# Load order, rank placement, first gates and gathers of a two-stage convolution block on one core

## The reference

```
y    = mean(gn(x)); gate = softmax(y Wg + bg)              # 8 experts
h    = relu(y W1 + b1); s = h W2 + b2
x    = x + gn(x) * sigmoid(sum_e gate_e s_e)               # a scale per image and channel

xz   = silu(in_proj(gn(x)));  x_ssm, res, gate = split(xz)
xf   = silu(depthwise_conv3(x_ssm))
perm = argsort(score) for each of 2 heads                  # a fixed order of the 1024 tokens
y    = selective_scan(gather(xf, perm), dt, A, B, C)       # dt, B, C from xf, gathered too
y    = gather(y, inverse perm)
x    = x + silu(out_proj(y * silu(gate) + res))
```

## Time and profile before

| | us |
|---|---|
| median of 3 runs | 946.37 (946.17 to 948.2) |
| profiled execution | 940.44 |
| its span in the trace | 938.6 |

### The profile page before, as it was taken

How to read it: one execution, slowest core, us unless ns; L and a number is a source line. 1 busy time by engine, 2 the same in 40 slices (tenths; PEclk the granted TensorE clock), 3 DMA queues, 4 the chain that set the end, 5 groups by cost and what they waited for, 6 DMA issues and landing times.

```text
span 938.6 us, 10961 instructions
## 1 busy us (share of the span) xinstructions
PE 790.8 (84%) x3732; PEld 508.5 (54%) x3732; DVE 580.3 (62%) x1112; ACT 563.7 (60%) x1069; POOL 344.3 (37%) x292
## 2 busy tenths in 40 slices
PE   1104888568999999999999999999999999977896
PEld 0003554466456745684568456755765566644753
DVE  6884614483759456864777476837692769267824
ACT  4850648343776486648754785578567756653452
POOL 0001224066504850385028621862086307530150
PEclk9655898688999999999999999999999999989899
DMA  8920005914785476637673759373937292757132
GB/s 304 412 84 0 1 32 146 121 51 147 191 108 205 152 194 81 221 121 219 81 225 129 207 83 232 128 209 74 234 129 209 73 159 87 213 127 142 55 126 90
DMA packets 109816, 136.10 MB, mean 145 GB/s; under 512 B 40761, under 2 KB 90434, under 8 KB 109762
## 3 DMA queue, kind: packets, MB, share of 16 engines
q1 hardware_dynamic: 97474, 99.61, 43.2%
q0 software_dynamic: 12288, 35.80, 11.6%
HBM read 82.83 MB, written 53.61 MB: 145 GB/s over the span
## 4 chain that ended last, share of the span: by engine, by line
PE 58%; ACT 13%; POOL 8%; DVE 7%; issue 7%; DMA 6%; SPq 2%; POOLq 0%; DVEq 0%; ACTq 0%
PE pj L1192 25%; PE pj L1314 7%; ACT big L522 5%; PE st L1234 5%; PE pj L1255 5%; POOL xt_scratch L396 4%; PE tp L1209 4%; PE tp L1211 3%; POOL crow L410 3%; PE pj L1265 3%; ACT xf L505 2%; DMA crow<-cd_scratch 2%; ACT L522 2%; DMA crow<-yt_scratch,idx 2%; PE tp L1304 2%
## 5 line engine op out<-in xcount | busy, mean ns | idle before, releaser
L1192 PE MATMUL pj<-xb,inw 128*128 128x512 f32 x768 | 339.7, 597 | 4.2 <-POOL xb L378 4.2
L396 POOL DMA_INDIRECT xt_scratch<-stage,idx x128 | 173.2, 1353 | 339.0 <-issue 267.3
L1192 PEld LDWEIGHTS pj<-xb,inw 128*128 128x128 f32 x768 | 143.3, 191 | 171.4 <-issue 163.7
L410 POOL DMA_INDIRECT crow<-yt_scratch,idx x128 | 133.2, 1040 | 139.3 <-DMA yt_scratch<-rs 57.7
L902 DVE SCALAR_TENSOR_TENSOR xf<-xs,small,xf 128x1024 f32<-128x1024 f32 x64 | 81.6, 1284 | 131.5 <-ACT xf L498 130.3
L1314 PE MATMUL pj<-gt,outw 128*128 128x512 f32 x256 | 118.1, 593 | 0.6 <-DVE gt L1056 0.6
L1255 PE MATMUL pj<-xp,mblk 128*128 128x128 f32 x512 | 72.7, 287 | 23.2 <-ACT gt L572 15.7
L545 ACT COPY ch<-tp 128x256 f32<-128x256 f32 x128 | 42.8, 381 | 82.2 <-PE tp L1246 82.0
L1255 PEld LDWEIGHTS pj<-xp,mblk 128*128 128x128 f32 x512 | 65.8, 201 | 29.4 <-ACT gt L572 21.5
L534 ACT COPY stage<-tp 128x256 f32<-128x256 f32 x128 | 47.9, 374 | 55.0 <-PE tp L1211 52.3
L1062 DVE SCALAR_TENSOR_TENSOR xb<-xb,pcur,rs 128x1024 f32<-128x1024 f32 x32 | 41.0, 1284 | 60.3 <-ACT rs L603 60.3
(11 more groups left out here) (191 smaller groups left out, 1138.9 us busy)
## 6 DMA issues: line engine op xcount, KB each, us to landing
xb<-in_x SPq DMA_DIRECT2D x26, 1024.0 KB, 8.7
xp<-xt_scratch SPq DMA_DIRECT2D x8, 2048.0 KB, 11.9
crow<-cd_scratch SPq DMA_DIRECT2D x64, 256.0 KB, 12.5
yt_scratch<-rs SPq DMA_DIRECT2D x16, 1024.0 KB, 4.9
out<-xb SPq DMA_DIRECT2D x16, 1024.0 KB, 7.4
xp<-xt_scratch SPq DMA_DIRECT2D x8, 272.0 KB, 8.7
xt_scratch<-stage,idx POOLq DMA_INDIRECT x128
crow<-yt_scratch,idx POOLq DMA_INDIRECT x128, 2.8
```

The lines of the kernel that those rows point to most:

```text
L396: pool.indirect_dma_start(out=xt_d.ap(), out_offset=bass.IndirectOffsetOnAxis(ap=idx[:, k:k + 1], axis=0), in_=v(stage, (nt * H + h) * ROW ...
L410: pool.indirect_dma_start(out=v(crow, k * NB * P, (1, NB * P)), out_offset=None, in_=yt_d.ap()[0:(h + 1) * N], in_offset=bass.IndirectOffs ...
L1192: last = nc.tensor.matmul(o[:, :], v(inw, ct * 3 * C + col + ot * P, (1, P)), x_view(par, b, ct, nt * HALF, HALF), start=(ct == 0), stop=( ...
```

## The change

- SP issues the loads of the first three pairs and of pair 3 ahead of seven small parameter loads, pair 4 ahead of the weights.
- DVE takes the statistics of pairs 0 to 3 before its first rank. Three of 16 ranks remain among the statistics, three in the setup chain, three stand behind `take_params` ahead of the first convolution, and seven behind both convolutions of pair 0.
- The negation of the decay constants moves from the statistics' end behind the softmax wait; ACT takes the square root of the first variance ahead of those constants' exponential.
- POOL no longer waits for `params_ready`. Pair 0 is scaled from `prm` as soon as scale and shift are written (a new semaphore, `scale_ready`); the other pairs read `pcur` as before.
- The gates of pair 0 move from the stretch ahead of cycle 0 into cycle 0, where those of other pairs stand in theirs. In cycle 7 ACT takes two gates ahead of the decays and two behind them.
- POOL issues the gathers of head 1 without waiting for those of head 0, and waits for both at the end.

The core of the diff; the matching lines on PE drop `if i:` in `cycle` and the two `gate(0, ...)` calls ahead of it, and the counts of DVE's setup steps at the end of the file are renumbered:

```diff
-            load_for_statistics(0)
+            for k in range(XB):
+                load_for_statistics(k)
+            load_for_statistics(XB)
...
-            load_for_statistics(1)
+            load_for_statistics(XB + 1)
...
-            for k in range(2, PH):
+            for k in range(XB + 2, PH):
                 load_for_statistics(k)
...
-            pool.wait_ge(params_ready, 1)
...
-                hold(pcur_ready, i + 1)
+                if i:
+                    hold(pcur_ready, i + 1)
+                else:
+                    hold(scale_ready, 1)
...
+                    params = v(pcur if i else prm, (par * NB + b) * PRM_W, (1, PRM_W))
...
-                hold(y_gathered[h], 128 * (i + 1))
+                if h == H - 1:
+                    hold(y_gathered[0], 128 * (i + 1))
+                    hold(y_gathered[1], 128 * (i + 1))
...
                 turned(i, 0, range(0, AHEAD))
-                decays(i, 1)
-                if i:
+                if more:
+                    decays(i, 1)
                     gate(i, par, range(0, 4))
-                turned(i, 0, range(AHEAD, 4 + AHEAD))
+                else:
+                    gate(i, par, range(0, 2))
+                    decays(i, 1)
+                    turned(i, 0, range(AHEAD, 4))
+                    gate(i, par, range(2, 4))
+                turned(i, 0, range(AHEAD if more else 4, 4 + AHEAD))
...
             rows_out(0, 0)
-            gate(0, 0, range(0, 4))
             convolved(0, 1)
             rows_out(0, 1)
-            gate(0, 0, range(4, 8))
-            for b in range(NB):
-                for ct in range(CT):
-                    gate_again(0, b, ct)
...
             statistics(2)
+            statistics(3)
...
-            for i in range(3, PH):
-                for _ in range(1 if i == 3 else 2):
+            for i in range(4, PH):
+                if i > 4:
                     rank(*next(tiles))
                 statistics(i)
...
-            nc.vector.tensor_tensor(per_image(PRM_B), v(dts, 192, (B, CT), (1, B)), v(dts, 128, (B, CT), (1, B)), ALU.mult)
+            nc.vector.tensor_tensor(per_image(PRM_B), v(dts, 192, (B, CT), (1, B)), v(dts, 128, (B, CT), (1, B)), ALU.mult).then_inc(scale_ready, 1)
...
+            for _ in range(3):
+                rank(*next(tiles))
             convolve(0, 0)
+            convolve(0, 1)
             for tile in tiles:
                 rank(*tile)
...
-            convolve(0, 1)
             add_bias(0, 0, 0, NT)
```

More of the change, by code:

```diff
@@ L195, in build @@
         z_ready = sem("z_ready")
+        scale_ready = sem("scale_ready")
         out_ready = sem("out_ready")
@@ L376, in scale_x @@
                     hold(x_in[par][b], x_loads(i))
+                    params = v(pcur if i else prm, (par * NB + b) * PRM_W, (1, PRM_W))
                     for ct in range(CT):
                         last = nc.gpsimd.tensor_scalar(x_view(par, b, ct), x_view(par, b, ct),
-                                                       v(pcur, (par * NB + b) * PRM_W + PRM_P + ct, (1, 1)),
-                                                       v(pcur, (par * NB + b) * PRM_W + PRM_B + ct, (1, 1)), ALU.mult, ALU.add)
+                                                       params[:, PRM_P + ct:PRM_P + ct + 1],
+                                                       params[:, PRM_B + ct:PRM_B + ct + 1], ALU.mult, ALU.add)
                     last.then_inc(x_scaled, 1)
@@ L463, in _ @@
                 statistics(i)
+            act.wait_ge(setup_v, V_VAR1)
+            did(nc.scalar.activation(v(dts, 0, (1, 32)), v(dts, 0, (1, 32)), ACT.Sqrt))
             act.wait_ge(weights_in, 15 * 16)
             did(nc.scalar.activation(v(small, ANEG, (1, 16)), v(small, ANEG, (1, 16)), ACT.Exp))
-            act.wait_ge(setup_v, V_VAR1)
-            did(nc.scalar.activation(v(dts, 0, (1, 32)), v(dts, 0, (1, 32)), ACT.Sqrt))
             act.wait_ge(setup_v, V_MAX)
@@ L618, in cycle @@
                 result(i, 0, 1)
-                if i:
-                    gate(i, par, range(4, 6))
+                gate(i, par, range(4, 6))
                 results(i, 1)
-                if i:
-                    gate(i, par, range(6, 8), TURNED)
-                    for b in range(NB):
-                        for ct in range(CT):
-                            gate_again(i, b, ct)
+                gate(i, par, range(6, 8), TURNED)
+                for b in range(NB):
+                    for ct in range(CT):
+                        gate_again(i, b, ct)
                 if beyond:
@@ L798, in _ @@
             link(nc.vector.scalar_tensor_tensor(col(SQ), col(SQ), 0.25, col(T), ALU.mult, ALU.add))
-            dve.wait_ge(setup_a, 3)
-            link(nc.vector.tensor_scalar(v(small, ANEG, (1, 16)), v(small, ANEG, (1, 16)), -1.0, None, ALU.mult))
             dve.wait_ge(stats_done_a, PH)
@@ L832, in _ @@
             dve.wait_ge(setup_a, 5)
+            link(nc.vector.tensor_scalar(v(small, ANEG, (1, 16)), v(small, ANEG, (1, 16)), -1.0, None, ALU.mult))
             link(nc.vector.reciprocal(v(bc8, 142, (1, 1), parts=B), v(bc8, 141, (1, 1), parts=B)))
@@ L1340, in cycle @@
                 before_t = (t_drained, i * T_U + AHEAD)
-                if i:
-                    gate(i, par, range(0, 4), last)
-                    last = four(g_drained, i * G_U + 4)
+                gate(i, par, range(0, 4), last)
+                last = four(g_drained, i * G_U + 4)
                 results(i, 0, before_t, last, AHEAD, lambda: chunk_sums(i, 1, 0))
                 last = four(r_drained, i * R_U + 4)
-                if i:
-                    gate(i, par, range(4, 6), last)
-                    last[:2] = four(g_drained, i * G_U + 8)[:2]
+                gate(i, par, range(4, 6), last)
+                last[:2] = four(g_drained, i * G_U + 8)[:2]
                 chunk_sums(i, 1, 1)
@@ L1351, in cycle @@
                 last = four(r_drained, (i + 1) * R_U)
-                if i:
-                    gate(i, par, range(6, 8), last, TURNED)
-                    last[:2] = four(g_drained, (i + 1) * G_U)[2:]
+                gate(i, par, range(6, 8), last, TURNED)
+                last[:2] = four(g_drained, (i + 1) * G_U)[2:]
                 last = last[TURNED:] + last[:TURNED]
@@ L1376, in _ @@
             rows(0, 0, None)
-            gate(0, 0, range(0, 4), four(a_drained, A_U))
             rows(0, 1, (x_drained, NT))
-            gate(0, 0, range(4, 8), four(g_drained, 4))
-            project(1, 0, four(g_drained, G_U))
+            project(1, 0, four(a_drained, A_U))
             project(1, 1, four(a_drained, A_U + 4))
@@ L1389 @@
 V_MOB = 6
-V_STATS = 54
-V_VAR1 = 58
-V_Y = 62
-V_MAX = 65
-V_HID = 69
-V_HIDT = 70
-V_STATS2 = 85
-V_VAR2 = 89
+V_STATS = 47
+V_VAR1 = 51
+V_Y = 55
+V_MAX = 58
+V_HID = 63
+V_HIDT = 64
+V_STATS2 = 79
+V_VAR2 = 83
 V_DIAG = 35
-V_Q = 92
+V_Q = 86
 P_EXPERT = 4
```

2 lines of the change are left out of this document (1 added, 1 removed).

## The result

The changed kernel takes **933.04 us** (median of 4 runs, 930.54 to 937.82) against 946.27 (944.59 to 948.2): ratio 0.987 [0.984, 0.990], 13.2 us less. The forecast was 925.2 with a range of 920 to 932.5: the sign was right, the gain was to be 21.15, and the time lies 0.5 above the range.

A forecast was written before the change was run, and what follows sets the result against it. Prediction: PE bounds the middle cycles, so gains come only elsewhere: 8.7 (loads and statistics) - 0.2 + 2.85 (setup) + 4.9 (into cycle 1) + 4.9 (last cycles) = 21.15; 946.37 - 21.15 = 925.2 us, range 920 to 932.5.

The forecast's parts named there:

- the loads: Loads for the statistics: new order fills 1.9 us of DMA holes, so the last half pair lands at 52.5, not 54.4.
- the last cycles: Cycles 6 and 7: 4.9 us (3 to 6), with 4.0 from head 1's earlier gathers in cycle 6, then 0.4 and 0.5.
- first projection to cycle 1: Stretch into cycle 0: gates moved and ranks redistributed end cycle 0 at 256.4 instead of 261.24, 4.9 us.
- rival 1: Loads: small ones cost DMA time wherever they stand, only DVE's lag goes, 6.7 for 8.7: 927.2 us; chance 0.12.
- DVE's lag: Statistics: DVE, 6.7 us behind the data because of nine rank steps, would with three be as early as the data.
- Setup: Before the first projection: pair 0 scaled once scale and shift are ready, PE starts near 89.9 instead of 92.72, 2.85 us.
- rival 3: Cycle 0: no room for the gates, all eight units, 15.8 us, come on PE's path after crow: 941.0; chance 0.06.
- rival 2: Pair 1's scaling: POOL and DVE exclude each other, 2.6 us delays the first convolution and scatter: 927.8; chance 0.10.
- the 0.4: Cycle 7: two gates ahead of the decays, so PE need not wait for their drains once the weights block is ready.
- The 0.5: Cycle 7's last gathers: PE waits 0.61 us there, so no more can come; 0.5 taken.
- Rival 4: Gathers: 16 in one go stall in POOL's descriptor writing or full DMA engines, losing 4.5 us: 929.7; chance 0.05.
- Rival 5: Every cycle: head 1's gathers beside DVE's taps hold DVE, 7.5 us per cycle, 27 over six cycles: 952; chance 0.03.

The follow-up runs named there:

- e5: The kernel before, unaltered, run again for a second trace: median 947.13 us, ratio 1.0005.
- after: The first profiled execution of the changed kernel: 930.54 us, span 928.4; its timed median is 933.04.
- e1: The changed kernel run again, unaltered: median 934.89 us, ratio 0.9862 to the kernel before.
- e4: The changed kernel with ACT's statistics of pair 2 moved ahead of its four score-row copies: median 933.32 us.
- e8: The changed kernel with pair 0's scaling again waiting for params_ready instead of scale and shift: median 937.42 us, ratio 0.9914 to the kernel before.
- e11: The changed kernel a third time, unaltered, on one chip with e9 and e10: median 939.66 us, ratio 0.9916 to the kernel before.
- e7: The changed kernel with pair 0's gates back in front of cycle 0: median 940.26 us, ratio 0.9934 to the kernel before.
- e3: The kernel before with only both heads' gathers issued in one go: median 948.59 us against 947.22, ratio 1.0022.
- e9: The changed kernel with the old wait between the heads' gathers in cycles 6 and 7 alone: median 937.05 us, ratio 0.9889 to the kernel before.
- e10: e6 with one go in cycles 0 to 5 and the old gather wait in 6 and 7: 934.75 us, ratio 0.9867 to the kernel before.
- e12: The changed kernel with the loads in the old order: median 940.89 us, ratio 0.9906 to the kernel before.
- e6: The changed kernel with the old gather wait, ACT's pair 2 statistics earlier, the 8-value load first, weights behind the last x load: 928.66 us, ratio 0.9816.

## Why the prediction was wrong

The size failed in two terms, the loads and the last cycles. The trace of e5 is the better measure for the stages than the first one, whose last cycle is untypical; its execution (942.79) still lies 4.3 under its median. Against it the three traces of the changed kernel end 12.4 earlier (941.0 against a mean of 928.6). By the columns of the table: landing -0.2, landing to first projection 9.25, first projection to cycle 1 4.5 (mean of 162.17, 161.42 and 164.36 against 167.14), cycle 1 to the end -1.1.

- **Loads, 1.9 forecast, -0.2 measured: failed.** Two steps of the sum were wrong. First, 0.9 of the 1.9 was read as a hole at 50 to 52.5, but there the loads run out: the engines are full until 51 and then ebb. The same ebb stands ahead of the landing in `after` and e1. Windows of the kernel before:

```profile
50.50:51.00 0.50, 0.00 (x0) 0.00 (x0) 0.50 (x1) 0.50 (x1) 0.00 (x0) 0.50 0.98 385
51.00:51.50 0.50, 0.00 (x0) 0.00 (x0) 0.50 (x3) 0.39 (x2) 0.00 (x0) 0.50 0.60 238
```

  Second, "the small ones no longer leave a hole": they take their time at another place. From 10 to 15 the loads went from 275 to 421 GB/s; from 25 to 30 they fell from 420 to 237 in `after`, and to 327 in e1. By the traces' DMA records the packets of 8 to 136 bytes moved along: 857 at 10 to 15 before, 836 and 896 at 25 to 30 in `after` and e1. In `after` the engines are idle for a part of it (shares 0.91 and 0.66), in e1 they are nearly full and yet move less. Windows of the kernel before, then of e1:

```profile
25.00:27.50 2.50, 1.41 (x4) 0.34 (x2) 0.78 (x2) 1.06 (x3) 0.00 (x0) 1.00 1.03 421
27.50:30.00 2.50, 0.00 (x0) 0.00 (x0) 1.30 (x3) 2.50 (x6) 0.00 (x0) 1.00 1.02 419
...
25.00:27.50 2.50, 1.80 (x5) 0.49 (x3) 2.50 (x5) 0.66 (x2) 0.00 (x0) 1.00 1.06 292
27.50:30.00 2.50, 0.00 (x0) 0.00 (x0) 2.40 (x14) 2.50 (x6) 0.00 (x0) 1.00 0.94 361
```

  So rival 1 gave the number and, in the main, the reason. Waits on the statistics stand there too: pair 4's load (24.84) waits for DVE's statistics of pair 1, which stand behind the second head's scores (the first four of the twelve at 22.34, to 24.8), and pair 5's (34.54) for ACT's of pair 2. But e4, which sends pair 5's load 2.9 earlier, lands no earlier. (The prediction has six half pairs ahead of the small loads; it is eight, and the last two wait for pair 0's statistics.) With the weights behind the last load, the landing does come earlier (51.76, 50.52).
- **DVE's lag, 6.8 forecast (8.7 less the landing's 1.9), 6.66 measured: right** (7.98 to 1.32 behind the landing).
- **Setup: right.** Scaling 2.97 (e8) for 2.85; the chain got longer by 0.4, not 0.2 (9.25 is 6.66 + 2.97 - 0.4).
- **First projection to cycle 1, 4.9 forecast, 4.5 measured: right in size, the parts not.** In the times of before (9.11 later, the difference of the first projections) the scatter starts at 130.15 (121.04 + 9.11) for 129.9 forecast. It then lost 2.5, not 0.3, beside taps, those of pair 1, and ACT's third copies, which waited 7.17 for it, began at 154.9 for 152.4. The crow load lands at 181.8 for 182.9, and DVE waits 2.40, not 7. The sentence that the gates cost nothing in cycle 0 holds; rival 3 (15.8 on PE's path) does not: PE's wait for the first weights block fell from 7.49 to 0.61, and cycle 0 takes 88.82, 88.74 and 91.02 with the gates (`after`, e1, e11), 89.06 without them in e7, and 89.39 and 87.11 in the kernel before. PE is busier by about 9 us there, at a granted clock of 0.91 for 0.83. Windows of cycle 0 in the kernel before, in `after` and in e7:

```profile
171.85:261.24 89.39, 71.75 (x365) 53.24 (x366) 55.45 (x96) 44.07 (x85) 43.03 (x36) 0.83 0.49 118
...
156.96:245.78 88.82, 80.68 (x397) 54.13 (x397) 55.24 (x96) 52.59 (x97) 46.06 (x36) 0.91 0.50 127
...
164.77:253.83 89.06, 71.17 (x364) 52.39 (x365) 55.33 (x96) 43.93 (x85) 44.63 (x36) 0.83 0.41 115
```

  So the gain is the gates', in the stretch ahead of cycle 0 that they left (e7).
- **POOL and DVE beside each other (rival 2): there, but hidden.** While POOL scales pair 1, two of DVE's three L785 take 0.53 and 1.11 where they take 0.35 elsewhere (so in all traces with ranks there, but for e8, which scales later), and POOL's four take 5.01 instead of 4.72:

```profile
84.84 0.53 DVE L785 SCALAR_TENSOR_TENSOR mblk<-crow,m,ch 128x128 f32<-128x128 f32 x1
...
86.75 1.11 DVE L785 SCALAR_TENSOR_TENSOR mblk<-crow,m,ch 128x128 f32<-128x128 f32 x1
...
91.58 2.61 DVE L906 SCALAR_TENSOR_TENSOR xf<-xs,small,xf 128x1024 f32<-128x1024 f32 x2 [1.71 <-ACT xf L505]
```

  DVE is idle for another 1.71 behind it, so 0.9 us of stretch costs nothing. The Trainium skill (SBUF — State Buffer, section "SBUF: two separate sides") has the two exclude each other for a whole instruction; the trace agrees in kind for these two, and the neighbouring L786 (0.34) was not held.
- **The last cycles, 4.9 forecast, -1.1 measured against e5: failed; this is the larger part.** The step "in cycle 6 ... I take 4.0 of the 4.52" holds for the gathers' start (4.3), not for what follows. In eight of eight traces with one go in cycle 6, DVE learns of PE's first turns 5.8 to 7.4 late, in six of six with the old wait within 0.4. From cycle 6's first L1224 to its first output pass 91.38 and 91.40 with one go (`after`, e1), 91.62 and 91.08 with the old wait (before, e5): what the earlier gathers win, the late signals take. Alone on the kernel before, one go costs 1.4 (e3). In cycle 7 the 0.4 came: PE's first products stand 34.53 behind the cycle's first row in `after`, 34.75 and 34.92 before, and follow the weights block at once. The 0.5 could not come: head 1's gathers there wait for head 1's store of y, in `after` (POOL's timeline) as in e5; the 4.46 of the earlier trace rows is the first trace's alone.

```profile
891.54 0.94 POOL L416 DMA_INDIRECT crow<-yt_scratch,idx  x1 [8.17 <-DMA yt_scratch<-rs]
```

  Rival 4 came near (929.7) with another mechanism: POOL's descriptor writing did not stall (0.94 to 0.95 for each gather of cycle 6).
- **The base: untypical, at a small price.** The sum was made against 940.44, and its cycle 7 was read for the 0.4 and 0.5 of the last term; the 0.5 fell with it. The trace is 4.1 us shorter in its tail than e5's. Carrying the 5.93 to the median kept the forecast's level right. But the gain between the two first traces (10.2) understates the change for that reason, and cycle 7's own loss looked like the change's.

Rival 5 (gathers hold DVE in every cycle) and a loss in the middle cycles did not come: 96.95. Of the prediction's signs of being wrong, the landing behind 54.4 came (54.52 and 55.02, but 53.26 in e1). The taps start 7.97, 7.74 and 7.33 behind the first projection, on both sides of its 7.6, as the two traces of the kernel before do (7.62 and 7.41).

**Open.** Why PE's signals come late. In `after` the eight turns of 806.88 and the four projections behind them end by 810, and their semaphore events appear together at 814.0 to 814.1, while landings of the gathers are recorded all through this time. In all eight traces with one go in cycle 6 DVE's late L1053 starts 0.1 to 1.7 us behind the last recorded landing of head 1's gathers, so by the records the signal came only when these were done. The ends of PE's rows in a trace are modelled, so a signal that came late and work that ended late look alike here. Cycle 3 takes 97.8 to 102.1 in every trace but the first of before, which has 96.94; in e9 ACT's copies and drains again run behind PE there. That is part of the spread between executions: e7, e9, e10 and e12, with 100.0 and more in it, have the four longest tails of the table. All these traces hold fewer semaphore events (6,620 to 7,448) than the first of before (9,484), and those with one go in cycles 0 to 5 the fewest (6,620 to 6,856). The Trainium skill (NOTIFIC — the notification-queue block, section "7.1 Overflow: three behaviours, one of which stalls the engine") says that the path of the profile's records can hold back an engine; no run here shows whether that is what happened. Also open is why the changed kernel spreads more by chip (933 to 940) than the kernel before (946 to 949).

## What to carry to other kernels

A wait that is taken away moves an edge; follow the edge to the next instruction that uses it, also in the stretch where it should be won, and price the stretch alone (here: the one edit on the kernel before) before it goes into a sum. Before a sum is made against one trace, take a second one and compare them stage by stage. How far an execution lies from the median does not tell: the first trace's lies 5.9 us under it and its cycle 7 is untypical, but e1's and e11's lie 6.3 and 6.6 under theirs with tails like the others'. A thin window at the end of the loads is their end, not a hole to fill; and a load that is moved takes its time along. When loads are reordered, list for each load the wait in front of it and what stands ahead of that wait on the engine that ends it. Taking bytes out from in front of the last load (e6 and e10, which have other edits too) went with an earlier landing; filling a hole did not.

## What was not expected of the hardware

- By the traces PE's work reached DVE 5.8 to 7.4 us and ACT 1 to 3.5 us late while POOL's gathers were under way, with the gathers' own landings recorded meanwhile.
- POOL's descriptor writes of the first scatter (POOL's timeline) stretch beside DVE's taps of pair 1, to 1.81 from 0.96 to 1.01, three times in 16, which is most of the 2.5 us that this scatter got longer:

```profile
127.97 1.81 POOL L402 DMA_INDIRECT xt_scratch<-stage,idx  x1 [0.30 <-issue]
130.08 1.01 POOL L402 DMA_INDIRECT xt_scratch<-stage,idx  x1 [0.30 <-issue]
131.40 1.82 POOL L402 DMA_INDIRECT xt_scratch<-stage,idx  x1 [0.30 <-issue]
```

- Between executions the last landing of 16 MB moved by up to 2 us (53.26 to 55.25 over seven traces with the same loads, on three chips), while everything from there to the first projection repeated within 0.03 (29.07 to 29.10 in the six of them that scale alike).
